# A DLRM tower on one core: 31 units per chunk instead of 32, an explicit order of TensorE's other work, the last chunk's layers handed over by block

## What is computed

```python
e = jnp.stack([tbl_0[ids[:, 0]], ..., tbl_31[ids[:, 31]]], axis=1)      # 512 x 32 x 64
pw = jnp.einsum('bpi,pij->bpj', e[:, ids_x, :], w)                      # 496 pairs, w is 496 x 64 x 64
z = jnp.einsum('bpj,bpj->bp', pw, e[:, ids_y, :])                       # 512 x 496
h = jnp.concatenate([z, dense_ctx], axis=1)                             # 512 x 512
h = jnp.maximum(h @ W_top1 + b_top1, 0.0)
h = jnp.maximum(h @ W_top2 + b_top2, 0.0)
y = h @ W_top3
```

## Time and profile before

| | |
|---|---|
| three executions | 263.15, 263.83, 263.94 us |
| median | 263.83 us |
| span of the profiled execution | 217.7 us |
| TensorE (PE) busy in it | 196.1 us, 90% |
| VectorE (DVE) busy | 174.1 us, 80% |
| ScalarE (ACT) busy | 150.4 us, 69% |
| GpSimd (POOL) busy | 150.2 us, 69% |

### The profile page before, as it was taken

One profiled execution on the slowest core, in us unless ns is written; L12 is line 12 of the kernel. 1 busy time (PEld: TensorE's weight loads), 2 busy tenths in 40 slices (PEclk: granted clock), 3 DMA queues, 4 the chain that ended last, 5 costly groups with the idle time before them and its releaser, 6 DMA issues.

```text
span 217.7 us, 6053 instructions
## 1 busy us (share of the span) xinstructions
PE 196.1 (90%) x2072; PEld 131.6 (60%) x2072; DVE 174.1 (80%) x159; ACT 150.4 (69%) x1146; POOL 150.2 (69%) x186
## 2 busy tenths in 40 slices
PE   0029899699999989999999999999999999999985
PEld 0007553575758549556786556865677755767874
DVE  0003789679999999999998999979989989897911
ACT  2010268299799957998199896599959978999201
POOL 4777777777777777777777777777788718777300
PEclk9999999969999999999999999999999999999999
DMA  5666656667111111111111111111110000000000
GB/s 190 252 222 223 230 205 223 218 215 229 30 25 29 35 24 29 29 24 32 25 27 32 27 24 34 25 29 30 29 27 6 2 3 0 2 5 0 3 0 3
DMA packets 6432, 15.21 MB, mean 70 GB/s; under 512 B 2689, under 2 KB 2945, under 8 KB 5250
## 3 DMA queue, kind: packets, MB, share of 16 engines
q1 hardware_dynamic: 2306, 10.62, 13.7%
...
...
## 4 chain that ended last, share of the span: by engine, by line
PE 79%; POOL 12%; issue 4%; DMA 3%; ACT 1%; DVE 0%; DVEq 0%
PE pu L485 25%; PE pu L477 24%; PE pz L498 13%; POOL emb L284 12%; PE pt L505 6%; PE pt L452 4%; PE pt L517 3%; DMA emb<-in_tbl,idx 3%; PE pu L505 1%; PE pt L527 1%; DMA idx<-in_ids 1%; PE pt L463 1%; PE pu L517 0%; ACT eT L303 0%; DVE zT L421 0%
## 5 line engine op out<-in xcount | busy, mean ns | idle before, releaser
L284 POOL DMA_INDIRECT emb<-in_tbl,idx x128 | 120.9, 945 | 41.1 <-issue 30.2
L312 ACT ACTIVATE turned<-turned 128x64 f32<-128x64 f32 x544 | 130.2, 245 | 1.5 <-DVE turned L389 1.5
L312 ACT ACTIVATION_READ_ACCUMULATOR turned<-turned 128x1 f32 x544 | 104.1, 191 | 0.0
L389 DVE TENSOR_TENSOR turned<-pu,emb 128x1024 f32<-128x1024 f32 x64 | 75.9, 1215 | 8.1 <-PE pu L477 7.8
L407 DVE TENSOR_TENSOR prod<-pu,eT 128x1024 f32<-128x1024 f32 x48 | 57.1, 1216 | 23.4 <-PE pu L485 23.3
L485 PEld LDWEIGHTS pu<-eT,ws 64*128 64x128 f32 x1024 | 64.9, 198 | 11.8 <-issue 10.4
L485 PE MATMUL pu<-eT,ws 64*128 64x128 f32 x1024 | 69.2, 287 | 0.0
L477 PE MATMUL pu<-ws,eT 64*128 64x512 f32 x256 | 65.5, 612 | 0.0
L303 ACT COPY eT<-pt 128x128 f32<-128x128 f32 (+1 forms) x28 | 11.2, 398 | 41.6 <-PE pt L452 41.6
L270 POOL TENSOR_TENSOR turned<-turned 128x512 f32<-128x512 f32 (+4 forms) x45 | 27.3, 607 | 11.4 <-DVE turned L389 8.4
L477 PEld LDWEIGHTS pu<-ws,eT 64*128 64x128 f32 x256 | 21.1, 186 | 16.7 <-issue 15.1
...
## 6 DMA issues: line engine op xcount, KB each, us to landing
...
emb<-in_tbl,idx POOLq DMA_INDIRECT x128, 2.4
...
w3s<-in_w SPq DMA_DIRECT2D x1, 1.0 KB
```

Of the source, the lines that this page charges most:

```text
L284: nc.gpsimd.indirect_dma_start(out=emb[:, c % EC, x, :], out_offset=None, in_=tables[x], in_offset=bass.IndirectOffsetOnAxis(ap=idx[:, c, ...
L312: i = nc.scalar.activation(t, t, ACT.Copy, accum_out=zB[:, b // NT % 2, b % NT * 16 + v:b % NT * 16 + v + 1])
L389: nc.vector.tensor_tensor(turned[:, b % RB, :, :].rearrange("p (x f) i -> p x (f i)", x=2), u.rearrange("p x s i -> p x (s i)"), e, ALU.mu ...
```

## The change

The pairs are divided into 31 units per chunk: the fourth kind of unit, "b", is gone, and three units c0, c1 and c2 take its pairs for all four groups of fields at once. They are turned units made of eight matmuls of 128 columns (weights of the array from eT, moving data from ws). Of the 31 units 16 stay turned, 15 are summed; the dense features now have only places of summed rows. NS is 124. The order of units is written out per chunk (UNIT_ORDER), and a row sum's number is now its place in that order. The tables X_AT, MLP_AT and SUMS_AT and the rule of two steps are replaced by one list, PLAN, that gives for each step what TensorE does behind it and in which order: "x" transposes, "s" one column sum, "z", "l1" (both halves of layer 1 at once), "l2", "l3". The second chunk's pairs are transposed in seven groups instead of four. Of the row sums, ScalarE gets 36 (34 before), VectorE 20 (21), GpSimd 8 (9). The last weight transfer has three units. In the last chunk all six column sums left stand behind the first part of layer 1, and the layers are handed on block by block with semaphores of their own (h1_last, h1_act, h2_last, h2_act, y_last). A path by which transposes could use the ring pu is added, but X_RING turns it off for all chunks.

```diff
...
+A_X = ((2, 5), (4, 7), (6, 7), (0, 1))
+C_X = {"c0": ((0, 3), (5, 3), 1), "c1": ((3, 1), (2, 5), 1), "c2": ((1, 0), (6, 3), 4)}
 UNITS = []
 for _j in range(KP // 4):
     UNITS += [("four", _k, 4 * _m) for _k in range(4 * _j, 4 * _j + 4) for _m in range(_j)]
-    UNITS += [("a", 4 * _j + 3, 4 * _j), ("b", 4 * _j + 3, 4 * _j)]
+    UNITS += [("a", 4 * _j + 3, 4 * _j)]
+UNITS += [(_c, KP - 1, 0) for _c in C_X]
 NU = len(UNITS)
 NS = BCH * NU
...
+TURNED = [4, 7, 10, 11, 12, 13, 15, 16, 17, 18, 24, 25, 26, 28, 29, 30]
...
-TURN_AT = [TURNED, [5, 6, 7, 8, 9, 14, 16, 17, 18, 19, 20, 21, 22, 23, 26, 29], [2, 6, 7, 8, 9, 10, 14, 16, 17, 22, 23, 24, 26, 27, 28, 30], [0, 5, 9, 10, 11, 13, 14, 15, 18, 19, 20, 22, 23, 24, 25, 26]]
...
+UNIT_ORDER = [[0, 1, 2, 3, 4, 7, 5, 6, 8, 10, 11, 15, 12, 17, 14, 18, 13, 20, 22, 23, 21, 19, 24, 30, 28, 25, 27, 16,
+               9, 26, 29],
...
+STEP_B = [_t for _t, _u in enumerate(ORDER) if _u in TURNED]
+STEP_A = [_t for _t, _u in enumerate(ORDER) if _u in SUMMED]
...
+Z_LAST = 123
...
-def slot_of(u, bank, slot):
+def slot_of(u, bank, slot, r):
     kind, k, m = UNITS[u]
     if kind == "four":
-        return k, m + slot, False
+        return 2 * k + bank, 2 * (m + slot) + r
     if kind == "a":
-        return m + (slot + 3) % 4, m + slot, False
-    x, y = STREAMS_B[bank][slot], bank + slot // 2 + slot % 2
-    return m + x, m + y, x == y
+        return 2 * m + A_X[slot][bank], 2 * (m + slot) + r
+    x, y = C_X[kind][bank]
+    return 8 * slot + x, 8 * slot + y + r * C_X[kind][2]
...
+X_SIZES = [[1, 1, 1, 1, 1, 1, 1, 1, 1, 1, 1, 1, 1, 1, 1, 1],
+           [4, 2, 2, 2, 2, 2, 2],
+           [4, 4, 4, 4],
+           [4, 4, 4, 4]]
...
-MLP_AT = [(7, 11, 20, 23, 30), (14, 16, 22, 29, 31), (14, 18, 22, 25, 27)]
...
-SUMS_AT = ((1, 4, 5, 9, 21, 29, 31), (1, 6, 8, 10, 17, 22), (2, 7, 11, 12, 27), (5, 9, 14, 27, 28, 31))
...
+PLAN = [(-1, 'x', 0), (-1, 'x', 1), (-1, 'x', 2), (-1, 'x', 3), (-1, 'x', 4), (1, 'x', 5), (1, 's', 0), (2, 'x', 6),
+        (2, 's', 1), (3, 's', 2), (3, 'x', 7), (3, 'x', 8), (6, 'x', 9), (6, 's', 3), (7, 's', 4), (7, 'x', 10), (9,
+        'x', 11), (10, 'x', 12), (10, 's', 5), (10, 's', 6), (11, 'x', 13), (14, 'x', 14), (17, 's', 7), (18, 'x',
...
+Z_OUT = [33, 65, 100]
...
+        L1_LAST = (0, 2, 1, 3)
...
-            for g in range(NU // WU):
+            for g in range(NW):
                 if g >= W_AT_ONCE:
                     sp.wait_ge(s_emb[2 * (g - W_AT_ONCE) + 1], 16 * 2)
-                sp.dma_start(ws[:, g * WU:(g + 1) * WU, :, :].rearrange("p u s i -> p (u s i)"),
-                             w[:, g * WU:(g + 1) * WU, :, :].rearrange("p u s i -> p (u s i)")).then_inc(s_w[g], 16)
+                sp.dma_start(ws[:, g * WU:min((g + 1) * WU, NU), :, :].rearrange("p u s i -> p (u s i)"),
...
-                        pool.wait_ge(u_ready, (c - 1) * NU + x + 1)
+                        pool.wait_ge(u_ready, (c - 1) * NU + min(x + 1, NU))
...
-            layer1(last, 0)
-            layer2(last)
-            layer3(last)
+            act.wait_ge(h2_ready, last)
+            for n in range(N1 // 2):
+                act.wait_ge(h1_last, L1_LAST.index(n) + 1)
+                nc.scalar.activation(h1[:, n, :], l1_out(last, n), ACT.Relu, bias=b1s[:, n:n + 1]).then_inc(h1_act, 1)
+            act.wait_ge(y_ready, last)
+            act.wait_ge(h2_last, 1)
+            nc.scalar.activation(h2[:, 0, :], l2_out(last, 0), ACT.Relu, bias=b2s[:, 0:1]).then_inc(h2_act, 1)
+            act.wait_ge(y_ready, BCH)
+            nc.scalar.copy(y[:, cols(last)], pt[0:1, 0, :]).then_inc(y_last, 1)
...
-            dve.wait_ge(h1_ready, 2 * BCH)
             for n in range(N1 // 2, N1):
+                dve.wait_ge(h1_last, L1_LAST.index(n) + 1)
                 nc.vector.tensor_scalar(h1[:, n, :], l1_out(last, n), b1s[:, n:n + 1], 0.0, ALU.add,
                                         ALU.max).then_inc(h1_dve, 1)
-            dve.wait_ge(h2_ready, BCH)
-            for n in range(N2 // 2, N2):
-                nc.vector.tensor_scalar(h2[:, n, :], l2_out(last, n), b2s[:, n:n + 1], 0.0, ALU.add,
-                                        ALU.max).then_inc(h2_dve, 1)
+            dve.wait_ge(h2_last, 2)
+            nc.vector.tensor_scalar(h2[:, 1, :], l2_out(last, 1), b2s[:, 1:2], 0.0, ALU.add, ALU.max).then_inc(h2_dve, 1)
...
+                if UNITS[u][0] in C_X:
+                    for slot in range(4):
+                        for bank in range(2):
+                            x = slot_of(u, bank, slot, 0)[0]
+                            rows = slice(EMB * (x % 2), EMB * (x % 2 + 1))
+                            i = nc.tensor.matmul(pu[:, unit_slot(t), bank, slot, :], eT[rows, c % EC, x // 2, :], ws[rows, u, slot, :],
+                                                 start=True, stop=True)
+                    i.then_inc(u_ready, 1)
+                    return
...
             pe.wait_ge(selected, 2)
-            for user in TURNS[-1]:
-                through_pt(*user)
-            for t in range(NS):
-                products(t)
-                for user in TURNS[t]:
-                    through_pt(*user)
-                for a in SUMS.get(t, ()):
-                    sums(a)
-            pt_free("l1a", last)
+            for t in range(-1, NS):
+                if t >= 0:
+                    products(t)
+                for extra in TURNS[t]:
+                    also(*extra)
+            pe.wait_ge(pt_read, len(USERS))
+            layer1(last, 0, Z_ORDER[:ZCH - ZA])
+            pe.wait_ge(mult_done, NS - 2)
+            for n in (2, 3):
+                layer1(last, n, Z_ORDER[:ZCH - ZA])
             pe.wait_ge(mult_done, NS - 1)
-            layer1(last, (0, 2, 3, 1), Z_ORDER[:ZCH - ZA])
-            for a in SUMS[NS]:
+            layer1(last, 1, Z_ORDER[:ZCH - ZA])
+            for a in range(len(SUMS), BCH * NA):
                 sums(a)
             pe.wait_ge(z_out, BCH)
-            layer1(last, range(N1), Z_ORDER[ZCH - ZA:])
-            through_pt("l2", last)
-            through_pt("l3", last)
+            for n in L1_LAST:
+                layer1(last, n, Z_ORDER[ZCH - ZA:]).then_inc(h1_last, 1)
+            for i in L1_LAST:
+                if i < N1 // 2:
+                    pe.wait_ge(h1_act, i + 1)
+                else:
+                    pe.wait_ge(h1_dve, i - N1 // 2 + 1)
+                for n in range(N2):
+                    mm = nc.tensor.matmul(l2_out(last, n), w2s[:, i, n * P:(n + 1) * P], h1[:, i, :],
+                                          start=(i == L1_LAST[0]), stop=(i == L1_LAST[-1]))
+                    if i == L1_LAST[-1]:
+                        mm.then_inc(h2_last, 1)
+            pe.wait_ge(h2_act, 1)
+            nc.tensor.matmul(pt[0:1, 0, :], w3s[:, 0:1], h2[:, 0, :], start=True, stop=False)
+            pe.wait_ge(h2_dve, 1)
+            nc.tensor.matmul(pt[0:1, 0, :], w3s[:, 1:2], h2[:, 1, :], start=False, stop=True).then_inc(y_ready, 1)
...
```

292 lines of the change are left out of this document (168 added, 124 removed), and 11 rows, old and new, of the table PLAN.

## The result

The changed kernel takes **266.94 us** (median; 265.84 to 268.28), the kernel before, run beside it, 263.88 us (263.15 to 264.08). The ratio is 1.0132, 95% interval 1.0104 to 1.0159: the change costs 1.3%. I had forecast 259.9 us, a gain of 1.5%, with the range up to 264.0.

The account below looks back on a forecast made before the run. TensorE was taken as the bound behind the gather phase. Terms -3.2 + 0.15 - 0.7 - 0.5 + 0.5 - 0.1 = -3.9 us took the median of 263.83 to 259.9 us, range 258.0 to 264.0.

Parts of the forecast that it names:

- The base: Whole kernel: profiled span 217.7 us, timed median 263.83; the 46.1 us outside the span were taken as untouched.
- What stands ahead of pair 13: First chunk, last pair TensorE waits for: work ahead of it is hidden by gathers, 15 units before, 12 after.
- Part 1: TensorE's units and column sums behind pair 13: fewer of them, units -0.62 us, sums -2.59, together -3.2.
- my prices: TensorE's pieces, from the chain: summed unit 0.89 us, turned unit 0.86, column sum 0.43, new kind taken as 0.89.
- Part 2: Explicit order behind pair 13: block switches +0.15 us; first chunk's z transposes no longer wait for ScalarE's copy, -0.7.
- Part 3: Weights: the eighth transfer is 768 KB instead of 1024, so pair 13 lands earlier, -0.5 us.
- Part 4: Last chunk: new wait for ScalarE's zT copy before layer 1, +0.5 us; handing layers over by block, -0.1.
- (b): Clock around pair 13: more TensorE idling makes the low clock last twice as long, +1.7 us, 261.6; chance 0.10.
- (c): VectorE becomes the bound, idling 2 us more where layer 1 stands in one piece: 263.6 us; chance 0.12.
- (d): Last two chunks: ScalarE's queue runs late, two row sums late give 267.1 us, slower; chance 0.13.

Follow-up runs that it names:

- changed, again: The changed kernel, unchanged, timed and profiled a second time on one chip with the kernel before: 265.96 us, span 263.9, ratio 1.0122.
- both second profiles: The kernel before and the changed kernel, both unchanged, timed and profiled again on one chip: 263.49 us (span 261.1) and 265.96 us (span 263.9).

## Why the new order loses more

**The tight places.** Column sums stand one step behind their unit in ten places; and joined layer 1 stands at the step behind which VectorE makes four row sums. GpSimd's and VectorE's timelines of the changed kernel, again:

```profile
134.88 4.59 DVE L492 TENSOR_REDUCE zB<-turned 128x16 f32<-128x1024 f32 x4
...
134.21 0.94 POOL L341 DMA_INDIRECT emb<-in_tbl,idx  x1 [0.30 <-issue]
138.54 0.94 POOL L341 DMA_INDIRECT emb<-in_tbl,idx  x1 [3.39 <-PE pu L585]
```

While VectorE sums rows it frees no PSUM bank, so TensorE finishes no unit, so GpSimd, which waits for a unit ahead of each gather, pauses 3.39 us. I read this as a chain of three engines: the pause comes when TensorE has no update to send, and the next updates fall into the next gathers. The kernel before has the same place in its third chunk (three row sums, a pause of 4.95 us ahead of the gather at 199.38), where the new order is 3.4 us shorter. Over the gathers of the third chunk (issued during the second) GpSimd's pauses over 0.5 us sum to 15.5 us before and 19.0 changed; over those of the fourth to 19.5 and 15.4.

Two edits loosen these places, apart and together. The first gives ten column sums a later step, the second splits layer 1 and the row sums:

```diff
+LATER = {0: 6, 1: 6, 2: 6, 4: 10, 11: 25, 22: 45, 28: 65, 34: 72, 38: 88, 50: 106}
```

```diff
-... (51, 'l1', 0) ... (80, 'l1', 1) ... (110, 'l1', 2)
+... (48, 'l1a', 0) ... (52, 'l1b', 0) ... (79, 'l1a', 1), (82, 'l1b', 1) ... (108, 'l1a', 2), (111, 'l1b', 2)
-('dve', 51), ('dve', 51), ('dve', 51), ('dve', 51)
+('dve', 46), ('dve', 48), ('dve', 50), ('dve', 52)
```

> The changed kernel with ten column sums moved to a later block, so that no sum stands directly behind the unit it sums (at least two steps, as in the kernel before; nine blocks had one step). Theory L (a sum that stands one step behind its unit waits for the round trip TensorE, VectorE, TensorE, and longer where TensorE's updates come late): 3 to 6 us faster than the changed kernel, so 260 to 263 us, and the first four sums no longer hold the standstill open. Rival (the loss is in ScalarE's fuller queue and the pair transposes): within 1 us of 266.

> The changed kernel with the joined layer 1 undone: its halves stand behind steps 48 and 52, 79 and 82, 108 and 111 instead of whole behind steps 51, 80 and 110, and the four row sums that VectorE makes behind step 51 stand behind steps 46, 48, 50 and 52. Nothing is left out. Theory V (VectorE's four row sums in a row, 3.5 us, with TensorE's 2 us of layer 1 behind them, are what the second chunk loses by): the second chunk takes 53 to 54.5 us instead of 57, and the kernel is 2 to 3.5 us faster than the changed one, 262.5 to 264.5 where that takes 266. Theory I (late updates slow every hand-over from TensorE to VectorE, wherever the row sums stand): second chunk 56 to 57 us, time within 1 us of the changed kernel's.

> The changed kernel, nothing left out, with both of its tight places loosened: layer 1 in halves and VectorE's four row sums apart (as in the split kernel), and ten column sums moved so that none stands right behind the unit it sums (as in the kernel with later sums). With the gathers of the last two chunks left out the changed order took 133.9 us from the second chunk's first product to the last one, the order before 137.6; with them 152.9 and 150.5. So the change gains 3.7 us and loses 6.1 more by late updates. Theory S (the loss comes from steps in which TensorE and VectorE depend on each other within one step; each loosened place gives back its part): 148 to 150 us for that stretch and a time 1 to 3 us below the changed kernel's, ratio to the kernel before 1.000 to 1.008. Rival T (it doesn't depend on these places; fewer other work between hand-overs is enough): 152 to 154 us, ratio 1.010 to 1.015.

| | ratio to before | second chunk | third | last |
|---|---|---|---|---|
| changed, again | 1.0122 [1.0072, 1.0172] | 57.0 | 52.1 | 43.8 |
| sums later | 1.0148 [1.0109, 1.0186] | 57.2 | 52.1 | 44.2 |
| layer 1 split | 1.0116 [1.0033, 1.0199] | 55.4 | 49.1 | 45.4 |
| both | 1.0084 [1.0043, 1.0124] | 56.1 | 50.0 | 45.8 |

Sums one step behind their unit are not the cause: theory L's 3 to 6 us lie outside the interval. The split takes the 3.39 us pause away (none over 2 us is left behind the first chunk) and 3.0 us from the three chunks of that profile, but most of it in the third chunk; the second, 55.4 us, lies between theory V and theory I, and the timed ratio can't be told from the changed kernel's. Both together take 151.9 us for the stretch, next to rival T's 152 to 154; the ratio lies between S and T, its interval touches either, and the medians alone (266.97 and 263.60 us) give 1.013. So that the joined layer and its row sums are one cause is a reading of the trace, which the times don't confirm, and it is not the whole.

**The rhythm of the gathers.** GpSimd waits ahead of each third (each second) gather, and then issues three (two):

```diff
-                    if c:
-                        pool.wait_ge(u_ready, (c - 1) * NU + min(x + 1, NU))
+                    if c and x % 3 == 0:
+                        pool.wait_ge(u_ready, (c - 1) * NU + min(x + 3, NU))
```

> The changed kernel, nothing left out. In the second to fourth chunks GpSimd no longer waits ahead of each gather for the unit of the same number in the chunk ahead; it waits ahead of each third gather until three more units are done, and then issues three. Theory B (TensorE's updates get through only in pauses of GpSimd of 0.8 us or more: in the second chunk of both kernels they came in groups of two and three, 0.8 to 1.3 us behind the end of a gather, while in the first profile of the kernel before they came 0.9 us apart, 29 of 37 during a gather; so a chunk under gathers costs 32 x 1.25 us and its pauses, and with three units done for each three gathers 4.7 to 5.2 us for three units): 49 to 54 us for the second chunk instead of 57, 49 to 53 for the third instead of 52, and 1 to 7 us less than the changed kernel in all. Rival P (what paces the chunk is TensorE's and VectorE's own order, and gathers only slow each hand-over): 55 to 59 and 51 to 54 us, time within 1.5 us of the changed kernel's.

> The kernel before, nothing left out, with the same bursts of three. By theory B its second chunk already runs in such groups (gathers come in twos and threes, 11 to 13 pauses of about 1.2 us): 50 to 54 us, and its third chunk loses the pauses of 3 and 5 us only in part: 52 to 56 us; time within 3 us of the kernel before. Rival P: 51 and 55.5 us, within 1 us of it.

> The changed kernel, nothing left out, with bursts of two gathers behind each two units. Theory B: more pauses, 16 a chunk, each of 1.2 us or more, so 2.5 + 1.2 us or more for two units: 58 to 64 us for the second and for the third chunk, and 3 to 12 us more than with bursts of three. Rival P: no difference to bursts of three beyond 1 us a chunk.

Measured, before at 260.75: threes 274.11 us, ratio 1.0483 [1.0386, 1.058], and on the kernel before 272.35 us, 1.0415 [1.0319, 1.0512]; twos 263.05 us (260.35 and 265.75). Nothing but the waits of one engine was changed, and both kernels lose 3.6 to 4.2 points. With threes the second chunk begins at 102.5 us (changed) and 101.2 (before) and takes 59.0 and 55.0; the third takes 51.4 and 58.4, the last 47.1 and 44.1. Rival P's ranges for the changed kernel's two chunks hold (those for the kernel before don't), but its time does not, by 8 us and more in both kernels: TensorE's and VectorE's own order alone doesn't pace them. Nor do the gathers come too late: behind the first chunk TensorE waits for no landing in either kernel. Theory B is right that the rhythm counts and wrong on its direction: it wanted threes to be best. With twos the second chunk takes 55.0 us, but that profile is of the slower of only two executions.

**All three together**: paced first chunk, split layer 1, bursts of two.

> The changed kernel, nothing left out, with the three additions that each shortened a stage in a run so far: the first chunk's gathers paced by ScalarE's copies (second chunk starts at 95.5 us instead of 98.9), the halves of layer 1 and VectorE's row sums apart (third chunk 49 us instead of 52.1), and bursts of two gathers behind the first chunk (second chunk 55.0 us instead of 57.1, third 50.1). Theory A (these gains add, since each ends another wait): second chunk starts at 95 to 97 us, 53 to 55 us for the second chunk, 47 to 49 for the third, 44 to 46 for the last, about 10 behind it: a span of 250 to 255 us and a ratio to the kernel before of 0.965 to 0.99. Rival C (GpSimd's gathers and the pauses that TensorE's updates need are one chain; what one edit wins, the next gather run takes back): span of 257 to 262 us, ratio 0.995 to 1.01.

Measured: 265.13 us (264.13 to 269.07), before 263.96, ratio 1.0059 [1.0021, 1.0098]. Step 4 came at 32.8 us and the second chunk at 97.2, but it took 57.6 us, the third 49.7, the last 46.8. Theory A's sum fell. Rival C's ratio holds, while its span (257 to 262 us for 263.3) is exceeded: the gains don't add. That a gather run and the updates that it holds up move on to the next place is how I read it; here 18 gathers without a pause, 38.4 to 60.6 us, go with VectorE idle until 61.2. No kernel with all its gathers was shown to beat the kernel before.

## Why the prediction was wrong, point by point

- **The base (the step that failed).** "263.83, 46.1 above the span; nothing in the change touches what lies outside the span" took an execution of 217.7 us for the timed ones. Of the 46 us, 43.4 lie inside the usual span: 30.5 up to the second chunk, 5.9 in it, 7.1 in the third (the table above), and there the change does act. So the sum had no term for what the gathers do to TensorE behind 42.33 us; it put that at nothing. Measured from the second chunk to the last product it is 12.9 us before and 19.0 us changed: 6.1 more, against a gain of 3.7, which is 2.4 of the 2.8 us between the spans. With the base went the argument that TensorE is the bound from 42.33 us on the earlier trace rows and over 99% busy behind 50 us: it is 89% in the changed kernel's second chunk (50.78 of 57.0).
- **What stands ahead of pair 13.** Its landing is not the last wait here. When the standstill ends, at about 50 us, all pairs are in, and the whole order behind step 3 is still to do.
- **Part 1.** About right as a sum, where it could be tried. Behind the first chunk my prices give three units less (-2.7), nine units of the new kind (+0.3), three or four column sums less (-1.5), and with the terms of parts 2 and 4 (-0.7, +0.15, +0.4) an estimate of about -4 us. Without gathers it was -3.4 (-3.7 up to the last product, +0.3 behind it), in one execution of each kernel. The new kind is a little dearer than I took: `pu L570` ran 192 pieces at a mean of 276 ns, and two units took 1.88 us in the chain at 86.17 us, against 2 x 0.89.
- **Part 2.** The first z transposes no longer wait: at 124.77 us they follow without a gap. True, and worth nothing while the gathers pace. "VectorE covers it with row sums of its own" is wrong under gathers: those row sums stand beside the 3.39 us pause.
- **Part 3.** The smaller last weight transfer can't be seen; no wait for pair 13 is left to shorten.
- **Part 4.** Right on the wait. The tail's chain, from the last z transposes; the new wait is 0.45 us (252.67 to 253.12) for my 0.5, and from the z transposes to the y copy it is 11.25 us against 10.97 before, where I had expected about 11.7:

```profile
252.29 0.38 PE pt L556 x2
...
252.70 0.38 ACT zT L384
...
253.12 0.71 PE pt L605 x4
...
263.29 0.25 ACT y L437
```

- **Rivals.** (b): the low clock is longer, a granted 0.57 from 20 to 50 us (0.94 in the first profile of before), but TensorE stands still there in both kernels, and from 50 to 55 us it is 0.50 in both second profiles. (c) and (d) name VectorE's cover and late row sums, and point at layer 1 in one piece, where the trace has the pause of 3.39 us; but the price, as I read the traces, came from a chain of three engines that I had not drawn, with GpSimd in it. I had taken GpSimd as fixed, since it "issues in the same number and order in both kernels". It does, but it waits for TensorE's units ahead of each gather, and holds TensorE up while it issues.
